# Fewer gathers in the first mixer's stage of a two-layer graph kernel, in bursts of four that wait until they have landed

## The reference, cut to what matters

```python
# graph part: attention over the edges that end in each node
e = leaky_relu(el[src] + er[dst], 0.2)
alpha = softmax of e over the edges of one dst, per head (4 heads)
rst = segment_sum(feat_src[src] * alpha, dst)      # 3125 x 256
# mixer: linear attention over all nodes
k = softmax(xn @ W_k, over the nodes); v = xn @ W_v
out = ((k^T v) per head) applied to q, then @ W_out
```

## Time and profile before

| what | before |
|---|---|
| median of 3 runs (lowest, highest) | 1989.68 us (1985.77, 1990.58) |
| span of the profiled execution | 2270.7 us |
| mean granted TensorE clock, share of full | 0.814 |
| PE, DVE, ACT, POOL busy in the span | 1595.3, 1257.2, 791.0, 1083.0 us |
| first mixer's stage | 122 to 216 us |
| first aggregation | 217 to 858 us |
| second aggregation | 1357 to 1990 us |

### The profile page before, as it was taken

The page is one execution under the profiler, slowest core; times in us unless marked ns, Lnnn a source line. Parts: engine busy times, 40 slices in busy tenths (PEclk is TensorE's granted clock), DMA queues, the critical chain, the costliest instruction groups (busy, mean ns, idle before and its releaser), DMA issues. The chain is left out here.

```text
span 2270.7 us, 31260 instructions
## 1 busy us (share of the span) xinstructions
PE 1595.3 (70%) x7757; PEld 1248.9 (55%) x7757; DVE 1257.2 (55%) x3845; ACT 791.0 (35%) x2693; POOL 1083.0 (48%) x1198
## 2 busy tenths in 40 slices
PE   5525566666775876969999756877777877974792
PEld 4523344444444545858888644655555654753692
DVE  3524465655655785736667635555454454676335
ACT  2212454645455674635666430000000000121351
POOL 2562666666666301312112156666566666236441
PEclk9655677777777798979999777887888888986896
DMA  5642444444444206445444223333232233122786
GB/s 183 212 137 63 126 122 124 137 119 127 132 124 121 82 3 226 138 135 164 153 153 153 79 80 107 90 93 87 80 91 84 84 91 92 41 75 82 211 263 216
DMA packets 176878, 276.88 MB, mean 122 GB/s; under 512 B 28920, under 2 KB 132218, under 8 KB 176456
## 3 DMA queue, kind: packets, MB, share of 16 engines
q0 software_dynamic: 50352, 136.58, 20.9%
q1 hardware_dynamic: 82610, 94.62, 13.5%
q10 hardware_dynamic: 43750, 43.75, 5.8%
HBM read 202.35 MB, written 73.58 MB: 122 GB/s over the span
## 5 line engine op out<-in xcount | busy, mean ns | idle before, releaser
L487 POOL DMA_INDIRECT ring<-feat_d,src_lane x440 | 434.4, 987 | 277.5 <-issue 122.3
L1207 POOL DMA_INDIRECT rows<-xn_d,src_of x416 | 404.6, 973 | 244.9 <-issue 115.2
L1187 PE MATMUL bank<-ring,a_hot 128*128 128x260 f32 x880 | 309.6, 503 | 174.9 <-DVE ring L1086 89.3
L1378 PE MATMUL bank<-rows,big 128*128 x880 | 290.0, 445 | 140.4 <-DVE big L1286 79.0
L1187 PEld LDWEIGHTS bank<-ring,a_hot 128*128 128x128 f32 x880 | 205.2, 249 | 245.8 <-DVE ring L1086 107.6
L1116 ACT ACTIVATE ring<-ring 128x64 f32<-128x64 f32 x1320 | 322.7, 336 | 8.1 <-issue 7.3
L1295 DVE TENSOR_TENSOR big<-bank,big 128x256 f32 x440 | 186.7, 424 | 232.1 <-DMA m_bo<-in_L_mix_bo 111.3
L1378 PEld LDWEIGHTS bank<-rows,big 128*128 128x128 f32 x880 | 163.7, 209 | 241.1 <-issue 227.0
L1071 DVE TENSOR_TENSOR acc<-bank,acc 128x260 f32 x440 | 186.5, 424 | 145.7 <-DMA m_dst_bc<-dst_lo_d 72.5
L1348 ACT ACTIVATE big<-bank,a_col 128x256 f32<-128x256 f32 (+1 forms) x26 | 13.0, 552 | 415.1 <-PE bank L1393 263.5
L1286 DVE TENSOR_SCALAR big<-const,dst_lane,ew_lane 128x128 f32<-128x128 f32 x440 | 153.6, 350 | 1.0 <-PEq L93 1.0
(11 more groups left out here) (399 smaller groups left out, 2912.8 us busy)
## 6 DMA issues: line engine op xcount, KB each, us to landing
slots_d<-fold ACTq DMA_DIRECT2D x25, 1300.0 KB, 5.6
e_w_now<-in_L_ffn_w SPq DMA_DIRECT2D x56, 256.0 KB
a_dst_bc<-dst_lo_d SPq DMA_DIRECT2D x23, 512.0 KB
big<-in_L_ffn_W SPq DMA_DIRECT2D x16, 512.0 KB
e_x<-slots_d SPq DMA_DIRECT2D x56, 130.0 KB
ring<-feat_d,src_lane POOLq DMA_INDIRECT x440
rows<-xn_d,src_of POOLq DMA_INDIRECT x416
e_ys<-y_d SPq DMA_DIRECT2D x24, 256.0 KB
```

The lines of the kernel that those rows point to most:

```text
L487: pool.indirect_dma_start(ring[:, q % RING, at, :], None, table, bass.IndirectOffsetOnAxis(ap=src_lane[:, n:n + 1], axis=0)).then_inc(gath ...
L1187: pe.matmul(bank[n % BANKS][:, 0:D + H], hot[:, q % HOTS, at, :], ring[:, q % RING, at, :], start=True, stop=True)\
L1207: pool.indirect_dma_start(rows[:, n % RING1, :], None, table, bass.IndirectOffsetOnAxis(ap=src_of[:, n:n + 1], axis=0)).then_inc(gathered[ ...
L1378: pe.matmul(bank[n % 4][:, 0:D], hot[:, n % HOTS, :], tile_of(rows, slots[n % 4]), start=True, stop=True)\
```

## The change

The first mixer's POOL program issues 20 gathers, steps 32 to 51, and not 42. Before each group of four it waits until the group of four before it has landed. The first aggregation begins its loop at step 52 and issues 388 gathers, which are the other 22 and the 366 that it had.

```diff
-BY_THEN = EARLY[NI + 1] + 42
+BY_THEN = EARLY[NI + 1] + 20

+def settled(pool, gathered, n):
+
+    q = n // 4
+    pool.wait_ge(gathered[q % RING], 16 * 4 * (q // RING + 1))

         # mixer_and_targets
         @block.gpsimd
         def _(pool):
             for n in range(EARLY[NI + 1], BY_THEN):
+                if n % 4 == 0:
+                    settled(pool, gathered, n - 1)
                 gather_rows(pool, ring, gathered, src_lane, feat_d, n)
```

## The result

The changed kernel takes 2013.80 us (median of 4 runs, 2009.85 to 2016.75) beside 1988.56 us for the kernel before (4 runs, 1985.77 to 1990.58). The ratio is 1.013, with a 95% interval from 1.0111 to 1.0149: 25 us slower. The forecast was 2001 us in a range from 1962 to 2018.

What follows compares the result with a forecast made beforehand. Stage order and waits bound the kernel, with POOL's gather issue setting the first aggregation. With s = 0.2, the mixer's -6.8 and the aggregation's +18.4 made +11.6 us, from 1989.68 to 2001 us; range 1962 to 2018.

Steps and rivals of the forecast that it cites:

- The mixer's late completions: First mixer: PE's completions reach other engines 6 to 33 us late while gathers issue back to back; idle times total 43.8 us.
- the share s: All gather stages: fraction of the late completions real in unrecorded runs; 0.2 taken, 0 to 1 kept open in the range.
- The 281 us between span and median: Whole kernel: profiled span exceeds the median run by 281 us, mostly attributed to late completions in the recorded execution.
- The stage sum with s = 0: Both mixers and aggregations: without late completions they would be 298 us shorter than profiled, against 281 observed.
- the first aggregation's loss: First aggregation: without late completions it would last 487 us against the profile's 641, 154 less.
- all of it is the recorder's: Rival: no late completions in unrecorded runs, so the change costs 24 us, 2014 us; slower by more than forecast, chance 0.24.
- POOL's line: First aggregation: gather issue at 1.258 us each sets its length, 487 us; 22 more gathers add 27.7 us, making 515.
- The mixer's gain at s = 0: First mixer without late completions: fewer gathers shorten the stage by 3.3 us.
- The bare chain: First mixer: the stage without its idle times, about 50 us.
- the waits would be hidden: First mixer: four landing waits of about 1.5 us; POOL ends some 31 us into the stage, inside 50.
- The slack at s = 1: First aggregation with fully real late completions: POOL's 83 us of slot waiting swallows most added gathers, leaving 11 us more.
- The price of the bursts of four: First mixer: twenty gathers in bursts cost between nothing and 0.51 us each, 10 us; upper end times s taken.

Runs made afterwards that it cites:

- light_before_c: Kernel before without ACT's weighing of the fourth head in the first aggregation, on a 1985 us chip: 1980.27 beside 1982.88 us, ratio 0.9988.
- free20_e: Kernel before with 20 mixer gathers back to back without waits, other 22 in the aggregation, on a 1985 us chip: 2010.15 beside 1982.88 us.
- changed_again: The changed kernel itself against the kernel before on a 2250 us chip: 2238.19 beside 2246.80 us, ratio 0.9973.
- free20: Kernel before with 20 mixer gathers back to back without waits, other 22 in the aggregation, on a 2250 us chip: 2251.25 beside 2249.88 us.
- free32: Kernel before with 32 mixer gathers back to back without waits, ten moved to the aggregation, on a 2250 us chip: 2245.24 beside 2249.88 us.
- before_third: Kernel before, nothing edited, profiled again on a 2250 us chip: 2250.49 beside 2250.03 us.
- paced42: Kernel before with all 42 mixer gathers kept, each group of four waiting for the last to land, on a 2250 us chip: 2230.18 beside 2249.88 us.

## Why the prediction was right or wrong

**The mixer's late completions**: read rightly in the profile that I had, and real there: with 42 gathers back to back the stage takes 93.6 to 94.4 us on the 2250 chips, with 20 paced ones 54.1. On the 1985 chips they do not occur: in each of the five profiles from 1985 chips all 25 turns of the stage are answered within 0.9 us of their start.

**The step that failed is the share s.** "So most of the late completions belong to the recorded execution. Call s the share of them that is real. With s = 0.2 ..." The 281 us between span and median were not stretched in by recording, since recorded executions on 1985 chips span about 1983 us, and s was no number to fit. The profile and the times were, as far as the stages tell, from different kinds of chip, one with s = 1 and one with s = 0. The stage sum with s = 0 came to 298 us for the 281 because it described the other kind of chip, but the excess of 17 us, from which the 0.2 was fitted, was no late completion. It was a sizing error: the first aggregation's loss was put at 154 us where the profiles (641 and 521.6) give 119, and some 25 us were missing elsewhere (light_before_c begins its mixer 15 us earlier, which was put at nothing, and its second mixer is 15 us shorter, which was put at 5). Taking 0.2 to close that gap cost 12 us of forecast, 11.6 where s = 0 gives 24 and 25 were measured, since between 0 and 0.25 the result falls from +24 to about 0. The rival "all of it is the recorder's" had the right number, +24 and 2014 us, for a reason that does not hold. That it met the 25 within 1 us is in part luck, as its terms were 1 to 3 us off each.

**POOL's line in the aggregation**: right as mechanism. The gathers' issue sets the stage, and 22 more cost 28.9 us (550.5 against 521.6, free20_e against light_before_c), where I had 27.7. The term is 1.31 us per gather and not 1.258. I had read the median, 953 ns, which is the same in both stages, but POOL's time goes by the mean, and that is 954 ns in light_before_c's mixer and 1001 in its aggregation. It could have been read in the profile of before (992 ns there). Why about a quarter of the aggregation's gathers take over 1 us no run shows. The line's total was short too, 487 where 521.6 was measured. 366 gathers took 477 us instead of 461, and behind the last one stood 44 us instead of 26, because not 6 groups but 11 are left then: a block's first group comes 21 to 23 us after its last gather is issued (free20_e, blocks 3 to 13), while its softmax bounds are found, and not right after the landing.

**The mixer's gain at s = 0**: forecast 3.3 us less, measured 0.5 to 0.7 less (53.3 and 53.1 against 53.8). The bare chain is 52 us and not the 50 that I got by adding up idle times. That the waits would be hidden was right, though they lasted 2.1 to 3.6 us and not 1.5.

**The slack at s = 1** was the other wrong term. I let POOL's 83 us of waiting swallow most of the 22 gathers and kept 11 us. Measured were 32.0 (changed_again), 30.2 (free20) and 12.6 for ten (free32). POOL's waiting did not shrink (80.7 to 78.5), and less weighing on ACT changed nothing that is clear of noise. One reading fits: the stops themselves are needed. POOL runs until the ring is full, PE's completions come when it stops, and this repeats at the same 1.48 to 1.49 us per gather whether 366 or 388 are issued. That reading is argued, not shown by a run of its own. A bound on DVE's or PE's side that grows with the gathers is its untested rival. The price of the bursts of four, where I took up to 10 us for twenty gathers, was about 1 us (54.1 in changed_again, 53.1 in the changed kernel on a 1985 chip).

## What to carry to other kernels

When a profile and the times differ by more than a per cent or two, they may show two machines and not one machine watched and unwatched: forecast each case whole, and don't fit a mixture. For an engine that sets the pace take the mean of its instructions in that stage, not the median. An issuing engine that runs back to back over several stages with a ring between it and its consumers is one long line, and work taken out of its idle-free stretch into a later stage comes back at its full issue price. A wait on that engine should be judged by whether it is idle behind it, and its idle time in an earlier stage (here 7 us in the middle and 7 us at the barrier) is the first place to put more of its work.

## What the runs showed of the hardware that had not been expected

On two kinds of chip the same program takes 1985 and 2250 us. The difference lies in the stages where POOL issues indirect DMAs one after another (second aggregation 530.4 and 620.7 us), and not in those without (280.5 and 279.8 us after it). In the mixer ACT answers a turn of PE up to 35 us after its start on the one kind (before_third) and within 0.9 us on the other. Pausing POOL for 2 to 4 us after every four gathers removes the delay: with all 42 gathers DVE's chain takes 52 us (paced42), and with 20 the stage takes 54.1 instead of 94.4 us, where 20 without pauses take 64.4. A pause stops POOL's issue and the gathers' data at once, so which of the two delays the completions is not shown. What differs in the chips was not found out.
